# Layer norm of a two-FFN block: normalisation and its preparatory steps on GpSimd in place of VectorE

## The reference

```python
x = x + 0.5 * ffn(layernorm(x))      # first feed-forward
x = x + mixer(layernorm(x))          # gated scan over the 1024 steps
x = x + 0.5 * ffn(layernorm(x))      # second feed-forward, same weights

def ffn(r):                          # its residual is the normalised input
    h = layernorm(r) * gamma + beta
    y = silu(h @ w1 + b1)            # w1: 256 x 1024, from integers and scales
    return r + 0.5 * (y @ w2 + b2)   # w2: 1024 x 256, from integers and scales
```

## Time and profile before

| | |
|---|---|
| median of 3 runs | 860.97 us |
| span of the profiled execution, first to last instruction | 856.8 us |
| TensorE matmuls busy | 811.6 us (95%) |
| VectorE busy | 808.8 us (94%) |
| ScalarE busy | 658.6 us (77%) |
| GpSimd busy | 558.6 us (65%) |
| chain that ended last | TensorE 81%, VectorE 11%, issue 4%, ScalarE 2%, GpSimd 1% |

### The profile page before, as it was taken

How to read it: one execution, slowest core, us unless ns; L and a number is a source line. 1 busy time by engine, 2 the same in 40 slices (tenths; PEclk the granted TensorE clock), 3 DMA queues, 4 the chain that set the end, 5 groups by cost and what they waited for, 6 DMA issues and landing times.

```text
span 856.8 us, 15154 instructions
## 1 busy us (share of the span) xinstructions
PE 811.6 (95%) x3682; PEld 624.0 (73%) x3682; DVE 808.8 (94%) x1645; ACT 658.6 (77%) x1083; POOL 558.6 (65%) x430
## 2 busy tenths in 40 slices
PE   1699999999999999999999998999999999999997
PEld 0477777777777778766777766777777777777785
DVE  4899999999999999979999997999999999999975
ACT  3488888888888888745655657888888888888884
POOL 4566777777667767735655656766677676776763
PEclk9999999999999999999999999999999999999999
DMA  8710000000000000000000000000000011000001
GB/s 258 236 48 2 2 0 0 0 0 0 0 0 0 0 0 1 2 1 1 0 0 0 0 1 1 0 26 25 24 24 24 24 35 38 25 24 24 26 25 50
DMA packets 20619, 20.33 MB, mean 24 GB/s; under 512 B 1590, under 2 KB 20332, under 8 KB 20588
## 3 DMA queue, kind: packets, MB, share of 16 engines
q1 hardware_dynamic: 19180, 17.86, 6.6%
q10 hardware_dynamic: 1312, 2.10, 0.7%
q0 software_dynamic: 96, 0.00, 0.0%
HBM read 11.57 MB, written 8.39 MB: 23 GB/s over the span
## 4 chain that ended last, share of the span: by engine, by line
PE 81%; DVE 11%; issue 4%; ACT 2%; DMA 1%; POOL 1%; DVEq 0%; ACTq 0%; POOLq 0%
PE ps_z L802 40%; PE ps_fc L802 26%; PE ps_fc L892 5%; PE ps_tr L795 3%; PE ps_tr L844 3%; DVE xhat L564 3%; DVE y_sb L587 2%; DVE z_acc L609 1%; PE ps_fc L900 1%; PE ps_fc L886 1%; DVE stats L537 1%; DMA resid<-in_L_attn_x 1%; DVE resid L578 1%; DVE resid L706 1%; PE ps_z L795 1%
## 5 line engine op out<-in xcount | busy, mean ns | idle before, releaser
L349 POOL TENSOR_TENSOR g_lo<-g_full,g_hi 128x512 fp32r<-128x512 f32 x256 | 334.9, 1308 | 187.5 <-ACT g_hi L463 181.1
L447 ACT ACTIVATE u_sb<-ps_fc,cols 128x512 f32<-128x512 f32 x256 | 199.0, 777 | 68.3 <-PE ps_fc L802 65.3
L802 PE MATMUL ps_fc<-h_hi,q_sb 128*128 128x512 f32 x512 | 218.2, 426 | 14.1 <-DVE y_sb L587 6.4
L802 PE MATMUL ps_fc<-h_lo,q_sb 128*128 128x512 f32 x512 | 204.0, 398 | 0.0
L609 DVE SCALAR_TENSOR_TENSOR z_acc<-ps_z,cols,z_acc 128x512 f32<-128x512 f32 x256 | 189.3, 741 | 11.1 <-PE ps_z L802 10.7
L587 DVE SCALAR_TENSOR_TENSOR y_sb<-ps_fc,cols,u_sb 128x512 f32<-128x512 f32 x256 | 189.3, 740 | 10.0 <-ACT u_sb L447 10.0
L461 ACT ACTIVATE g_full<-y_sb 128x512 f32<-128x512 f32 x256 | 159.7, 624 | 37.6 <-DVE y_sb L587 37.6
L564 DVE TENSOR_SCALAR xhat<-resid,mean_var,rstd 128x256 f32 (+1 forms) x192 | 167.3, 917 | 3.3 <-POOL rstd L335 3.3
L463 ACT ACTIVATE g_hi<-y_sb 128x512 fp32r<-128x512 f32 x256 | 158.5, 619 | 0.0
L802 PEld LDWEIGHTS ps_fc<-h_hi,q_sb 128*128 128x128 f32 x512 | 97.2, 190 | 49.0 <-DVE y_sb L587 24.3
L802 PE MATMUL ps_z<-g_hi,q_sb 128*128 128x512 f32 x288 | 116.8, 405 | 3.0 <-DVE z_acc L607 2.6
(11 more groups left out here) (97 smaller groups left out, 1164.4 us busy)
## 6 DMA issues: line engine op xcount, KB each, us to landing
resid<-in_L_attn_x SPq DMA_DIRECT2D x16, 512.0 KB, 4.2
out_x<-resid SPq DMA_DIRECT2D x16, 512.0 KB, 2.9
q_int<-in_L_ffn_fc_q ACTq DMA_DIRECT2D x2, 1024.0 KB, 8.8
z_acc<-in_L_ffn_fc_scales SPq DMA_DIRECT2D x1, 256.0 KB, 8.0
wd_sb<-in_L_attn_Wd SPq DMA_DIRECT2D x1, 256.0 KB
z_acc<-in_L_ffn_fc_scales SPq DMA_DIRECT2D x1, 192.0 KB, 8.6
resid<-in_L_attn_Wy SPq DMA_DIRECT2D x2, 64.0 KB
wab_sb<-in_L_attn_Wa SPq DMA_DIRECT2D x1, 64.0 KB
```

Source lines behind the costliest of these rows:

```text
L349: nc.gpsimd.tensor_tensor(g_lo[:, slot % 4, :], g_full[:, slot % 2, :], g_hi[:, slot % 4, :].bitcast(F32), ALU.subtract).then_inc(g_ready, 1)
L447: nc.scalar.activation(u_sb[:, f % 2, :], ps_fc1[:, f % 2, 0, :], ACT.Identity, bias=col(R_B1 + f), scale=col(R_S1 + f)).then_inc(u_ready, 1)
L802: last = nc.tensor.matmul(out, w, v, start=start and i == 0, stop=stop and i == len(pairs) - 1)
```

## The change

The four `normalise` operations of every layer norm and the operations on `var_terms` move from VectorE to GpSimd. GpSimd has no subtraction of the mean in the new form, so a `neg_mean` is made first. `rsqrt` on GpSimd is now: the variance terms, `neg_mean`, a wait on its own `terms_ready`, the power. It moves from f = 2 to f = 3; `normalise` is at f = 4 and 5 (5 and 6 in the first tile). `residual` stays on VectorE, moves from f = 6 to f = 7 and waits for `xhat_ready`. In the mixer GpSimd normalises after its two `xn_low`. GpSimd's tiles are all written out (`each_tile`); the other engines keep their loop.

```diff
@@ -44,9 +44,9 @@
...
-    RSQRT_AT = 2
-    NORMALISE_AT = ((4, 5), (6, 7))
-    RESIDUAL_AT = (6, 7)
+    RSQRT_AT = 3
+    NORMALISE_AT = ((4, 5), (5, 6))
+    RESIDUAL_AT = (7, 7)
@@ -104,6 +104,7 @@
...
+        neg_mean = sb("neg_mean", [P, SUB])
@@ -266,6 +267,12 @@
...
+
+        def each_tile(tile):
+
+
+            for t in range(NT):
+                tile(t, t % 2, min(t, 2), min(NT - 1 - t, 2))
@@ -329,11 +336,34 @@
...
-            def rsqrt(ln, n):
-
-                pool.wait_ge(var_ready, ln + 1)
+            def rsqrt(ln, twice):
+
+                pool.wait_ge(aggr_done, ln + 1)
+                wait(pool, xhat_ready, ln)
+                nc.gpsimd.tensor_scalar(var_terms[:, 0:SUB], mean_var[:, :, 1], EPS, 1.0, ALU.add, ALU.mult)
+                if twice:
+
+
+                    nc.gpsimd.tensor_scalar(var_terms[:, SUB:2 * SUB], mean_var[:, :, 1], 1.0 + EPS,
+                                            EPS * EPS, ALU.mult, ALU.add)
+                nc.gpsimd.tensor_scalar(neg_mean[:, :], mean_var[:, :, 0], -1.0, 0.0, ALU.mult,
+                                        ALU.add).then_inc(terms_ready, 1)
+                pool.wait_ge(terms_ready, ln + 1)
+                n = 2 * SUB if twice else SUB
                 nc.gpsimd.tensor_tensor(rstd[:, 0:n], var_terms[:, 0:n], minus_half[:, 0:n],
                                         ALU.pow).then_inc(rstd_ready, 1)
+
+            def normalise(ln, t, twice, blocks=range(SUB)):
+
+                if blocks[0] == 0:
+                    pool.wait_ge(rstd_ready, ln + 1)
+                    wait(pool, turned, 2 * ln)
+                at = SUB if twice else 0
+                for a in blocks:
+                    last = nc.gpsimd.tensor_scalar(xhat[:, a, :], resid[:, t, a, :], neg_mean[:, a:a + 1],
+                                                   rstd[:, at + a:at + a + 1], ALU.add, ALU.mult)
+                if blocks[-1] == SUB - 1:
+                    last.then_inc(xhat_ready, 1)
@@ -359,10 +389,7 @@
...
-                if type(t) is int and t == NT - 1:
-                    pool.wait_ge(h_ready, 2 * NT + 2)
-                else:
-                    pool.wait_ge(xn_ready, 2 * t + 4)
+                pool.wait_ge(xhat_ready, t + (NT + 3))
                 nc.gpsimd.tensor_tensor(cs_parts[N:2 * N, par, :], cs_full, cs_parts[0:N, par, :].bitcast(F32),
                                         ALU.subtract).then_inc(cs_lo_ready, 1)
                 pool.wait_ge(cs_lo_ready, t + 1)
@@ -377,21 +404,27 @@
...
-                        if f == RSQRT_AT and (behind >= 2 or ff0 == 0):
-                            rsqrt(ln + 2, 2 * SUB if behind >= 2 else SUB)
+                        if behind >= 2 or ff0 == 0:
+                            t2, twice = (t + 2, True) if behind >= 2 else (1 - behind, False)
+                            if f == RSQRT_AT:
+                                rsqrt(ln + 2, twice)
+                            if f in NORMALISE_AT[not before]:
+                                normalise(ln + 2, t2, twice, halves[NORMALISE_AT[not before].index(f)])
                 if ff0 == 0:
-                    rsqrt(ln0, 2 * SUB)
+                    rsqrt(ln0, True)
+                    normalise(ln0, 0, True)
...
                     pool.wait_ge(s2_loaded, 16 * KC)
                     pool.wait_ge(w2_int_ready, KC)
                     nc.gpsimd.tensor_tensor(w2_full, w2_full, s2_wide, ALU.mult).then_inc(w2_full_ready, 1)
-                    rsqrt(ln0 + 1, 2 * SUB)
+                    rsqrt(ln0 + 1, True)
+                    normalise(ln0 + 1, 1, True)
                     pool.wait_ge(w2_hi_ready, 1)
                     nc.gpsimd.tensor_tensor(w2_lo[:, :, :], w2_full, w2_hi[:, :, :].bitcast(F32),
                                             ALU.subtract).then_inc(w2_ready, 1)
-                over_tiles(pool, tile)
+                each_tile(tile)
@@ -399,13 +432,15 @@
...
-                rsqrt(t + (NT + 2), SUB if behind >= 2 else 2 * SUB)
+                twice = behind < 2
+                rsqrt(t + (NT + 2), twice)
                 for c in range(KC):
                     if behind:
                         xn_low(t + 1, 1 - par, c)
                     else:
                         h_low(2 * NT, NT, 0, c)
-            over_tiles(pool, mixer_tile)
+                normalise(t + (NT + 2), 1 - behind if twice else t + 2, twice)
+            each_tile(mixer_tile)
@@ -538,37 +573,19 @@
...
-            def variance(ln, twice):
+            def variance(ln):
 
                 dve.wait_ge(stats_done, ln + 1)
+                wait(dve, terms_ready, ln)
                 nc.vector.memset(wait_holder[:, :], 0.0)
                 for a in range(SUB):
                     last = nc.vector.bn_aggr(mean_var[:, a, :], stats[:, a, :])
                 last.then_inc(aggr_done, 1)
-                dve.wait_ge(aggr_done, ln + 1)
-                last = nc.vector.tensor_scalar(var_terms[:, 0:SUB], mean_var[:, :, 1], EPS, None, ALU.add)
-                if twice:
-
-
-                    last = nc.vector.tensor_scalar(var_terms[:, SUB:2 * SUB], mean_var[:, :, 1], 1.0 + EPS,
-                                                   EPS * EPS, ALU.mult, ALU.add)
-                last.then_inc(var_ready, 1)
-
-            def normalise(ln, t, twice, blocks=range(SUB)):
+
+            def residual(ln, ff, t, blocks=range(SUB)):
 
                 if blocks[0] == 0:
-                    dve.wait_ge(rstd_ready, ln + 1)
...
-            def residual(ff, t, blocks=range(SUB)):
-
-                if blocks[0] == 0:
+                    dve.wait_ge(xhat_ready, ln + 1)
                     nc.vector.tensor_scalar(res_scale[:, :], rstd[:, 0:SUB], 0.5, 1.0, ALU.mult, ALU.add)
                     nc.vector.scalar_tensor_tensor(out=res_shift[:, :], in0=mean_var[:, :, 0], scalar=-0.5,
                                                    in1=rstd[:, 0:SUB], op0=ALU.mult,
@@ -637,7 +654,7 @@
                             for half in range(2):
                                 add_mixer(NT - 1, 1, half)
                         if behind >= 1 and f == 0:
-                            residual(ff + 1, t + 1, range(2, SUB))
+                            residual(ln + 1, ff + 1, t + 1, range(2, SUB))
                         if ff0 == 0 and not before and f == 3:
                             prepare_mixer()
                         if behind >= 2 or ff0 == 0:
...
-                                variance(ln + 2, twice)
-                            if f in NORMALISE_AT[not before]:
-                                normalise(ln + 2, t2, twice, halves[NORMALISE_AT[not before].index(f)])
+                                variance(ln + 2)
                             if f == RESIDUAL_AT[not before] and twice:
-                                residual(ff + 2, t + 2, range(2))
+                                residual(ln + 2, ff + 2, t + 2, range(2))
                         if before and f in ADD_AT:
                             add_ffn(ff - 1, t - 1, ADD_AT.index(f))
 
                 if ff0 == 0:
...
-                    variance(ln0, True)
-                    normalise(ln0, 0, True)
+                    variance(ln0)
                     largest_of(0, q1_sb, q1_ready, 1)
                     largest_of(1, q2_sb, q2_ready, KC)
                     find_width()
-                    residual(ff0, 0)
+                    residual(ln0, ff0, 0)
...
-                    variance(ln0 + 1, True)
+                    variance(ln0 + 1)
                     dve.wait_ge(w2_full_ready, 1)
                     nc.vector.tensor_copy(w2_hi[:, :, :], w2_full).then_inc(w2_hi_ready, 1)
-                    normalise(ln0 + 1, 1, True)
-                    residual(ff0 + 1, 1, range(2))
+                    residual(ln0 + 1, ff0 + 1, 1, range(2))
@@ -755,17 +768,10 @@
...
-                    variance(t + (NT + 2), twice)
+                    variance(t + (NT + 2))
                 scan(t, par)
                 dve.wait_ge(c_part_ready, t + 1)
                 nc.vector.tensor_tensor(c_sum, ps_c[0:N, :], c_part, ALU.add).then_inc(c_sum_ready, 1)
-                def norm():
-                    normalise(t + (NT + 2), t2, twice)
-                    if twice:
-                        residual(NT + t2, t2, range(2 if t2 else SUB))
-
-                if behind:
-                    norm()
...
                 nc.vector.tensor_tensor(cs_full, c_sb[:, par, :], state[:, par, :], ALU.mult).then_inc(cs_ready, 1)
-                if not behind:
-                    norm()
+                if twice:
+                    residual(t + (NT + 2), NT + t2, t2, range(2 if t2 else SUB))
...
```

More of the change, by code:

```diff
@@ L183, in macaron_kernel @@
         aggr_done = sem("aggr_done")
-        var_ready = sem("var_ready")
+        terms_ready = sem("terms_ready")
         rstd_ready = sem("rstd_ready")
@@ L547, in variance @@
                 last.then_inc(aggr_done, 1)
-                dve.wait_ge(aggr_done, ln + 1)
```

(22 more changed lines are left out.)

## The result

The changed kernel takes 1000.55 us (median of 4 runs, 998.02 to 1005.27), the kernel before it 860.99 beside it: a ratio of 1.1634, with a 95% interval of 1.1604 to 1.1665. The prediction was 896, range 845 to 912. The direction was right, the size was not: +140 us instead of +35.

What follows compares the result with a forecast made beforehand. It took TensorE to lead, with VectorE also full and weight loads waiting for y_sb. Span 856.8 + 34 (feed-forward stalls) + 1 (ends), mixer 0, gave 892; the median stands 4.2 above, so 896 us, range 845 to 912.

Steps and rivals of the forecast that it cites:

- first-order reading: Feed-forward: the residual on VectorE waits for GpSimd's g_lo and delays TensorE; +1.23 us a tile, +34 us over 28 tiles.
- E: Feed-forward tile: end of GpSimd's normalisations, counted from the start of f = 2; claimed at 15.6 us.
- R: Feed-forward tile: end of the residual on VectorE, 18.7 us with two locks or 19.65 with three.
- three locks: Residual at f = 7: res_scale and both first-pair residuals each wait for a g_lo; stall 2.0 us, against 1.1 with two.
- the 1.9 us that I had forecast: TensorE's stall in each feed-forward tile, taken in the middle of 1.1 and 2.75 us; period 21.83 against 20.60.
- the deadline: Feed-forward: TensorE needs y_sb(1) at f = 3 of the next tile, 22.26 us, with 4.62 us of VectorE's queue ahead.
- t: Length of one 128x256 normalisation on GpSimd: taken as 0.47 us, bounded by 0.31 and 0.80.
- cover of 3.52 us: Mixer: GpSimd's idle time before cs_low would take in its new work, so the mixer was costed at 0.
- X: GpSimd's three preparatory operations before the power: taken as 0.6 us, between 0.3 and 0.9.
- The start: First layer norm, serial at the kernel's beginning: +0.9 us, taken as +1 for the ends.
- The residual escapes: Rival, feed-forward: normalisations end before VectorE arrives, stall 0 to 0.4 us; 842 to 853 us, if X + 4t is below 2.2; chance 0.33.
- GpSimd becomes the bound: Rival, feed-forward: at t = 0.80 the stall is 3.3 us and more, silu waits on g_lo; some 935 us; chance 0.06.

Runs made afterwards that it cites:

- Experiment 1: Changed kernel with the residual's four operations and its two small ones left out, the wait for xhat_ready kept: 844.0 us.
- experiment 2: Changed kernel with the residual's operations replaced by bn_stats of the same blocks and a small memset, behind the same wait: 863.31 us.
- Experiment 13: Small separate kernel that only copies x; one VectorE operation is issued just after GpSimd began n g_lo-like operations back to back: 67.23 us.
- experiment 4: Changed kernel with TensorE computing the group at which it stands six more times into the same bank: 957.8 us.
- experiment 8: Changed kernel with the residual at f = 1 and 2 of the next tile and the mixer's four normalisations back on VectorE: 866.85 us.
- Experiment 9: Changed kernel with the residual at f = 1 and 2 of the next tile and the mixer's normalisation and variance terms back on VectorE: 850.49 us.
- experiment 5: Kernel before the change with only GpSimd's tiles written out instead of looped: 860.53 us against 860.92.
- experiment 3: Changed kernel with res_scale and res_shift made on GpSimd, the four residual operations kept on VectorE: 986.46 us.
- experiment 10: Same kernel as Experiment 9 but with the residual at f = 0 and 1 in place of f = 1 and 2: 886.02 us.

## Why the prediction was wrong

**Right.** The first-order reading held: the residual that stays on VectorE, moved into GpSimd's dense stretch, is locked out once for res_scale and again for the pair, and what is queued behind it stops TensorE. From E, the end of the normalisations, to R, the end of the residual, I had 4.05 with three locks; the trace has 207.34 - 203.15 = 4.19. The three g_lo were right, how they are shared out was not: I had one for res_scale and one for each residual of the pair; it is two for res_scale (or one for it and one for res_shift, which I had left out) and one for the first residual, while the second runs free. So the close agreement is partly luck. Experiment 1 removes the loss with the residual, experiment 2 keeps its work without the lock. In the Trainium skill (SBUF — State Buffer, "Who interferes with whom") the second to issue is blocked until the first finishes, for VectorE in a 2-port mode or with two SBUF inputs. Experiment 13 agrees for the rows shown (1.21 held, 0.43 not); the kernel's 2.51 is longer than that sentence allows, and there the measurement decides.

**Wrong, the largest term: TensorE's clock.** The sum priced a stall at its own length. A stall of 3.4 us also put TensorE at 0.50 of its clock (1.2 GHz), for some 6.8 us in one tile and about half of that in the next (means of 0.87 and 0.93 over the tiles). The tile of 26.14 lost 2.8 us to it; experiment 4, where it doesn't happen, is 43 us faster. Of the 146.7 us some 63 are the clock by an estimate from these rows (28 tiles, 2.8 and 1.7 in turn), some 75 the stall itself (3.4 less the 0.67 of before), 10 the mixer and the start. In the Trainium skill (TensorE: Matmul & The Clock Gate, Part 1) an idle TensorE is put to half clock and activity releases it. The trace agrees in the tile shown; in the next the clock fell only after TensorE had started again. The term hangs on the others: at the 1.9 us that I had forecast no run shows the clock falling, and the single stall of 2.10 us that ends at 44.27 left it at 1.00. So the term may be there only because the stall was longer than forecast; a stall of 2 us in every tile was not tried.

**Wrong, the deadline.** I had TensorE stop for y_sb(1) at f = 3 of the next tile, 22.26 from the start of f = 2, with 4.62 us of VectorE's queue ahead of it. It stops earlier, for the bank that the first z_acc behind the residual must empty: in the same frame at 18.56 (205.34 is 18.6), with add_ffn and z_acc, 1.33, ahead. By my own R of 19.65 that is 19.65 + 1.33 - 18.56 = 2.4 us against 2.0. The wait for that very bank was hidden before, but its kind was in the trace: the view of the earlier trace rows has this line too, a wait in nearly every tile, which I passed over:

```profile
PEld ps_z L802 <- DVE z_acc L609: 13.5, 31, 2.1
```

The code shows it as well: each group of the second layer waits for the bank of an older one.

**Mis-sized terms, 1.0 us together.** E was 16.45 in that frame, not 15.6. A pair of normalisations took 1.06 to 1.10 (t = 0.53 to 0.55, not 0.47), the three preparatory operations 221.75 - 220.95 = 0.80, not 0.6. The remaining 0.4 lies in what stands ahead of them. R was 20.64, and the stall 20.64 + 1.33 - 18.56 = 3.4. So of the 6.2 us by which this tile is above 19.93, 2.0 were in the prediction (three locks), 0.4 were the deadline, 1.0 R, 2.8 the clock.

**The mixer.** Costed at 0 under a cover of 3.52 us; it cost 7.8. GpSimd is busy 28.82 us of 30 there and hardly idles in a tile, so by the rows it is the bound (TensorE's 29.98 hides its waits, since the ends of matmuls are modelled; 134 start, not the 136 of the earlier trace rows). X and 4t weren't 2.5 us: the variance term stood for 0.51, neg_mean for 1.18, the two xn_low for 2.95 (2.54 in experiment 8), the first two behind VectorE by the rows, and 2.16 for the normalisation. That is the lock in the other direction, which the prediction left out. Experiment 9 shows that the price is that of the layer norm on GpSimd: with all of it back on VectorE the mixer is 138.2. How it divides between load and waits isn't shown; in experiment 8 GpSimd has less to do, idles 3.4 us a tile, and the mixer is longer still. The start was +2.2 where I took +1; written-out tiles cost nothing (experiment 5).

**The rivals.** "The residual escapes" fell with t = 0.53 and X = 0.8: X + 4t = 2.9 is above its 2.2. But its gain is there once the residual stands elsewhere. "GpSimd becomes the bound" fell for the feed-forwards (experiment 1: 844 with all of its load), and in the mixer the rows speak for it. Nearest in size was the 935 of that rival, for the wrong reason.

## What to carry to other kernels

When work moves from VectorE to GpSimd, look first at the operations from SBUF to SBUF that stay on VectorE and at what GpSimd queues around them: here the kernel took 1000.55 us with them in its dense run and 858.95 with them in its gaps; with the mixer's layer norm back on VectorE, 886.02 at the edge of the run and 850.49 in the gaps. Price a stall of the matmul engine by its clock too, once it comes near the 3.1 to 3.4 us at which the clock fell here in most tiles. And for each thing that gets late, list all that the next engine needs of it, its buffers to be emptied as well as its data, and take the earliest.

## What the runs showed of the hardware

- TensorE's granted clock fell to 0.50 at about 207.9, 2.6 us after the last matmul had ended, and stayed there until 214.7, though TensorE was busy again from 208.73; matmuls of 128x512 started 0.43 apart in place of 0.233. In the next tile TensorE stood for 3.2 us, and the clock fell only when it was running again, for half as long. In experiment 3 stalls of 3.1 us brought it down in some tiles and not in others. Waits of 0.5 us (experiment 4) and 1.1 us (experiment 10) left it at 1.00.
- Between VectorE and GpSimd the wait goes both ways: GpSimd's 128x4 operation takes 0.20 alone and up to 1.18 under VectorE's scan, VectorE's takes 0.15 alone and 1.21 under a g_lo, and 2.51 in most tiles of the kernel after, 1.26 in the others.
- A tensor_scalar on GpSimd with scalars from SBUF takes 0.53 us for 128x256 from start to start (1.06 for two), less than half of a two-input operation of twice the columns (1.27).
